# A three-layer interaction network with an MLP on one Trainium2 core: products and sums of layer 0 spread over four tiles, MLP parts known early moved ahead, and a head issued from two queues

## The reference

```python
def _cin_layer(X0, Xi, W, b):
    H = W.shape[0]
    F0_, Fi = (X0.shape[1], Xi.shape[1])
    Wr = W.reshape(H, F0_, Fi)
    return jnp.einsum('hjk,bjd,bkd->bhd', Wr, X0, Xi) + b[None, :, None]
...
e = jnp.stack([tbl_0[ids[:, 0]], ...], axis=1)      # (512, 39, 16)
X0 = Xi = e
for W, b in Ws:
    Xi = _cin_layer(X0, Xi, W, b)
    res.append(Xi.sum(axis=2))
z = jnp.concatenate(res, axis=1)                      # (512, 384)
h = jnp.concatenate([z, dense_ctx], axis=1)
h = jnp.maximum(h @ W_top1 + b_top1, 0.0)
h = jnp.maximum(h @ W_top2 + b_top2, 0.0)
y = h @ W_top3
```

## Time and profile before

| | us |
|---|---|
| median of three runs | 722.71 |
| the profiled execution, as timed | 718.87 |
| its span in the trace | 717.1 |
| TensorE busy | 671.6 (94%) |
| ScalarE busy | 541.1 (75%) |
| VectorE busy | 469.7 (66%) |
| GpSimd busy | 460.5 (64%) |

### The profile page before, as it was taken

How to read it: one execution, slowest core, us unless ns; L and a number is a source line. 1 busy time by engine, 2 the same in 40 slices (tenths; PEclk the granted TensorE clock), 3 DMA queues, 4 the chain that set the end, 5 groups by cost and what they waited for, 6 DMA issues and landing times. The chain is left out here.

```text
span 717.1 us, 10090 instructions
## 1 busy us (share of the span) xinstructions
PE 671.6 (94%) x2631; PEld 481.9 (67%) x2631; DVE 469.7 (66%) x954; ACT 541.1 (75%) x1939; POOL 460.5 (64%) x445
## 2 busy tenths in 40 slices
PE   4597999999999999999999999999999999998998
PEld 4464777777677767676767677776777776774443
DVE  6245677778677777777676777786777777784000
ACT  4255797979797979888897979797979798993003
POOL 6765686877778686868686868777785736321000
PEclk9699999999999999999999999999999999998999
DMA  6664040404031312213040404040313122300000
GB/s 202 220 176 97 1 99 1 98 1 98 2 95 6 92 8 73 26 41 59 16 84 3 98 2 97 2 97 3 96 4 93 5 79 91 143 1 0 0 1 0
DMA packets 103772, 41.40 MB, mean 58 GB/s; under 512 B 86961, under 2 KB 90033, under 8 KB 103074
## 3 DMA queue, kind: packets, MB, share of 16 engines
q1 hardware_dynamic: 98594, 39.47, 21.7%
q0 software_dynamic: 5120, 1.29, 2.2%
HBM read 11.29 MB, written 2.59 MB: 19 GB/s over the span
## 5 line engine op out<-in xcount | busy, mean ns | idle before, releaser
L415 ACT ACTIVATE prod<-ps_y,xt 128x128 f32<-128x128 f32 x1792 | 498.1, 452 | 88.0 <-PE ps_y L659 79.4
L657 PE MATMUL ps_y<-w_hi,x_hi 128*128 128x512 f32 (+1 forms) x640 | 307.9, 481 | 16.2 <-DVE prod L529 14.4
L323 POOL TENSOR_TENSOR prod<-prod 128x512 f32<-128x512 f32 x128 | 165.6, 1294 | 133.6 <-ACT prod L415 132.0
L659 PE MATMUL ps_y<-w_hi,x_lo 128*128 128x512 f32 (+1 forms) x640 | 249.2, 389 | 0.0
L658 PE MATMUL ps_y<-w_lo,x_hi 128*128 128x512 f32 (+1 forms) x640 | 248.9, 389 | 0.0
L529 DVE SCALAR_TENSOR_TENSOR prod<-ps_y,xt,prod 128x128 f32<-128x128 f32 x576 | 163.8, 343 | 48.0 <-PE ps_y L659 46.2
L298 POOL DMA_INDIRECT rows<-in_table,index x160 | 153.4, 959 | 42.7 <-issue 35.7
L657 PEld LDWEIGHTS ps_y<-w_hi,x_hi 128*128 128x128 f32 x640 | 120.8, 189 | 72.3 <-DVE prod L529 26.3
L536 DVE TENSOR_REDUCE prod<-prod 128x128 f32<-128x1536 f32 x64 | 112.2, 1753 | 85.3 <-ACT prod L415 53.0
L658 PEld LDWEIGHTS ps_y<-w_lo,x_hi 128*128 128x128 f32 x640 | 120.8, 189 | 47.1 <-issue 25.5
L659 PEld LDWEIGHTS ps_y<-w_hi,x_lo 128*128 128x128 f32 x640 | 120.5, 188 | 25.3
(11 more groups left out here) (62 smaller groups left out, 235.9 us busy)
## 6 DMA issues: line engine op xcount, KB each, us to landing
room<-room SPq DMA_DIRECT2D x80, 234.0 KB
room<-room SPq DMA_DIRECT2D x48, 78.0 KB
emb_room<-rows SPq DMA_DIRECT2D x180, 5.0 KB
rows<-in_table,index POOLq DMA_INDIRECT x160
g_all<-in_L_rec_W SPq DMA_DIRECT2D x1, 2496.0 KB, 9.8
room<-room SPq DMA_DIRECT2D x16, 156.0 KB
w2t_dram<-g_all SPq DMA_DIRECT2D x1, 2496.0 KB
room<-w2t_dram SPq DMA_DIRECT2D x1, 2496.0 KB, 8.9
```

The source lines that it names most:

```text
L323: nc.gpsimd.tensor_tensor(prod[:, SLOT[a]:SLOT[a] + 2], prod[:, SLOT[a]:SLOT[a] + 2], prod[:, SLOT[b]:SLOT[b] + 2], ALU.add).then_inc(pool ...
L415: ins = nc.scalar.activation(prod[:, SLOT[k] + m // 2, :, m % 2], ps_y[:, g % YBANKS, m * H:(m + 1) * H], ACT.Copy, scale=xt[:, q % 2, ti, ...
L657: nc.tensor.matmul(y, hi, w1_hi[:, cols], start=True, stop=False)
L659: nc.tensor.matmul(y, lo, w1_hi[:, cols], start=False, stop=True).then_inc(y_made, 1)
```

## The change

- **Layer 0 beside the tiles.** The seven sums on TensorE were one in tile 1, five in tile 2 and one in tile 3; now they are one, two, two and two. GpSimd's products move ahead with them, the first two into tile 0. Four gathers of tile 0 are spread over tiles 0 to 2. The shares have a semaphore of their own, so the first product waits for them alone.
- **Tail.** Two of the four parts of the first MLP layer need nothing of layer 1. They now have their accumulators in four banks. For two of these the matmuls go behind group 3 of tiles 60 to 63, for the two others right behind tile 63. The part with layer 1's output goes behind the 39 matmuls with W2. The second layer runs both halves for three inputs first and then for the fourth. The bias of `r1` is added after tile 60.
- **Head.** ScalarE's queue issues half of the first lay-outs, shares and windows. W2 is loaded in two parts, the first ahead of the small loads, and turned in three lots: five groups before the rows are turned, three after, two behind layer 0. GpSimd repeats the rows of quad 1 ahead of the last three gathers of quad 2.

```diff
-MULTIPLIED_IN = {(1, 0): range(0, 1), (1, 1): range(1, 4), (2, 0): range(4, 5), (2, 1): range(5, CHUNKS)}
-GATHERED_IN = {(0, 0): range(0, 1), (0, 1): range(1, 5), (3, 0): range(5, 6), (3, 1): range(6, GATHERS)}
+MULTIPLIED_IN = {(0, 1): range(0, 2), (1, 0): range(2, 3), (1, 1): range(3, 4), (2, 0): range(4, 5),
+                 (2, 1): range(5, CHUNKS)}
+GATHERED_IN = {(0, 0): range(0, 1), (0, 1): range(1, 2), (1, 1): range(2, 4), (2, 1): range(4, 5),
+               (3, 0): range(5, 6), (3, 1): range(6, GATHERS)}
 REPEATED_IN = (2, 1)
-SUMMED_AFTER = {(1, 8): 0, (2, 0): 1, (2, 2): 2, (2, 4): 3, (2, 6): 4, (2, 9): 5, (3, 1): 6}
+
+SUMMED_AFTER = {(0, 9): 0, (1, 4): 1, (1, 9): 2, (2, 3): 3, (2, 8): 4, (3, 0): 5, (3, 2): 6}
 SUM_D_AFTER = 6
+
+MLP_AFTER = {(0, 3): (0, 0), (1, 3): (1, 0), (2, 3): (0, 1), (3, 3): (1, 1)}
...
+PREP_EARLY = PREP - PREP_W2 + PREP_W2 // 2
+PREP_LATE = PREP - 2
...
+        ps_h1 = [ps_tr[:], ps_x1[:], ps_y[:, 0, :], ps_y[:, 1, :]]
+        ps_r3 = ps_y[:, 2, :]
+        ps_h2 = [ps_y[:, 3, :], ps_y[:, 4, :]]
+        ps_out = ps_g[0:1, :]
...
+            sp.dma_start(w2_in[:, W1_PARTS[0]], W2[:, W1_PARTS[0]]).then_inc(w2_ld[0], 16)
...
-            lay_out(0)
-            sp.dma_start(w2_in, W2).then_inc(w2_ld, 16)
+            lay_out(0, range(FPG // 2))
+            sp.dma_start(w2_in[:, W1_PARTS[1]], W2[:, W1_PARTS[1]]).then_inc(w2_ld[1], 16)
+
             sp.wait_ge(x0_made, 1)
-            share_rows(0, first_shared)
-            for c in range(1, CHUNKS):
-                cut_window(0, c, first_window[c])
-            lay_out(1)
+            share_part(sp, 0, 0, first_shared)
+            share_part(sp, 0, 2, first_shared)
+            for c in range(2, CHUNKS, 2):
+                cut_part(sp, 0, c, first_window[c])
+            lay_out(1, range(FPG // 2))
...
             def multiply(q, c):
                 if c == 0:
-                    wait(pool, shifted[q % 2], 16 * MOVES * ((q + 1) // 2))
+                    wait(pool, shared[q % 2], 16 * SPC * ((q + 1) // 2))
+                    wait(pool, z_used, CHUNKS * (q - 1) + 1)
+                if c == 1:
+                    wait(pool, cut[q % 2], 16 * (CHUNKS - 1) * ((q + 1) // 2))
                 r = chunk_rows(c)
                 window = bz[0:r, c, :] if c else x0[0:r, q % 2, :]
-                if c == 0:
-                    wait(pool, z_used, CHUNKS * (q - 1) + 1)
                 nc.gpsimd.tensor_tensor(bz[0:r, c, :], window, xa[0:r, :], ALU.mult).then_inc(z_made, 1)
...
             for g in range(GATHERS):
+                if g == GATHERS - 3:
+                    repeat_rows(1)
                 gather(2, g)
-            repeat_rows(1)
...
+            act.wait_ge(gathered[0], 16 * GATHERS)
+            for f in range(FPG // 2, FPG):
+                lay_out_part(act, 0, f)
+            for n in range(PREP - PREP_W2, PREP_EARLY):
+                keep_prep(n)
             keep_x0(0)
+            act.wait_ge(x0_made, 1)
+            share_part(act, 0, 1, first_shared)
+            for c in range(1, CHUNKS, 2):
+                cut_part(act, 0, c, first_window[c])
             keep_xt(0)
-            for n in range(PREP - PREP_W2, PREP):
+            for n in range(PREP_EARLY, PREP_LATE):
                 keep_prep(n)
+            act.wait_ge(gathered[1], 16 * GATHERS)
+            for f in range(FPG // 2, FPG):
+                lay_out_part(act, 1, f)
             keep_x1(0)
+            for n in range(PREP_LATE, PREP):
+                keep_prep(n)
...
+                if T == TILES - QT:
+                    dve.wait_ge(bsum_made, 1)
+                    dve.wait_ge(r1_made, QUADS)
+                    nc.vector.tensor_scalar(r1[:], r1[:], b02_sum[:, 0:1], None, ALU.add).then_inc(r1_done, 1)
             reduce_late(TILES - 1)
-            dve.wait_ge(bsum_made, 1)
-            dve.wait_ge(r1_made, QUADS)
-            nc.vector.tensor_scalar(r1[:], r1[:], b02_sum[:, 0:1], None, ALU.add).then_inc(r1_done, 1)
...
-            for n in range(PREP - PREP_W2):
+            for n in range(PREP_EARLY):
                 turn_prep(n)
             turn_rows(0)
             turn_x(0)
-            for n in range(PREP - PREP_W2, PREP):
+            for n in range(PREP_EARLY, PREP_LATE):
                 turn_prep(n)
             for c in range(CHUNKS):
                 layer0(0, c)
+            for n in range(PREP_LATE, PREP):
+                turn_prep(n)
```

On TensorE, the new function and the tail:

```diff
+            def known_mlp1(m, part):
+                if (m, part) == (0, 0):
+                    pe.wait_ge(late_mlp, 64)
+
+                    pe.wait_ge(bd_made, QUADS)
+                    pe.wait_ge(x1_lo_made, QUADS)
+                    pe.wait_ge(r1_made, QUADS)
+                if (m, part) == (0, 1):
+                    pe.wait_ge(r1_done, 1)
+                w, z = (wt1[0:C, 3, m * P:(m + 1) * P], dense_t[:]) if part == 0 else (wt1[:, 0, m * P:(m + 1) * P], r1[:])
+                nc.tensor.matmul(ps_h1[m], w, z, start=part == 0, stop=False)
...
-            def mlp1(c, rows_c, z, start, stop):
-                for m in range(MC1):
-                    ins = nc.tensor.matmul(ps_y[:, m, :], wt1[0:rows_c, c, m * P:(m + 1) * P], z,
-                                           start=start, stop=stop)
-                    if stop:
-                        ins.then_inc(h1_summed, 1)
-
-            pe.wait_ge(late_mlp, 64)
-            pe.wait_ge(act_step, ACT_STEPS * TILES)
-            pe.wait_ge(dve_step, DVE_STEPS * TILES)
-            mlp1(3, C, dense_t[:], True, False)
-            pe.wait_ge(r1_done, 1)
-            mlp1(0, P, r1[:], False, False)
+                    if not nxt and (ti, g) in MLP_AFTER:
+                        known_mlp1(*MLP_AFTER[ti, g])
+
+            for m in range(2, MC1):
+
+                if m == 2:
+                    pe.wait_ge(dve_step, DVE_STEPS * (TILES - 1) + DVE_DONE[YBANKS])
+                else:
+                    pe.wait_ge(act_step, ACT_STEPS * (TILES - 1) + ACT_GROUPS.index(YBANKS + 1) + 1)
+                for part in range(2):
+                    known_mlp1(m, part)
             sum_d(TILES - 1)
             pe.wait_ge(late_w2, 16)
             pe.wait_ge(g_kept, TILES)
-            mlp1(1, P, g_all[:, F, :], False, False)
+            pe.wait_ge(act_step, ACT_STEPS * TILES)
             for j in range(F):
-                ins = nc.tensor.matmul(ps_x1[:], w2t[:, j * H:(j + 1) * H], g_all[:, j, :],
-                                       start=j == 0, stop=j == F - 1)
+                ins = nc.tensor.matmul(ps_r3, w2t[:, j * H:(j + 1) * H], g_all[:, j, :], start=j == 0, stop=j == F - 1)
             ins.then_inc(r3_summed, 1)
+            for m in range(MC1):
+                nc.tensor.matmul(ps_h1[m], wt1[:, 1, m * P:(m + 1) * P], g_all[:, F, :], start=False, stop=False)
             pe.wait_ge(r3_made, 1)
-            mlp1(2, P, r3, False, True)
-            for m in range(MC2):
-                dst = ps_y[:, YBANKS - 1, :] if m == 0 else ps_g[:]
-                for c in range(MC1):
-                    if m == 0:
-                        pe.wait_ge(h1_made, c + 1)
-                    ins = nc.tensor.matmul(dst, wt2[:, c, m * P:(m + 1) * P], h1[:, c, :],
-                                           start=c == 0, stop=c == MC1 - 1)
-                ins.then_inc(h2_summed, 1)
+            for m in range(MC1):
+                nc.tensor.matmul(ps_h1[m], wt1[:, 2, m * P:(m + 1) * P], r3, start=False,
+                                 stop=True).then_inc(h1_summed, 1)
+            for half in (range(MC1 - 1), range(MC1 - 1, MC1)):
+                for m in range(MC2):
+                    for c in half:
+                        if m == 0:
+                            pe.wait_ge(h1_made, c + 1)
+                        ins = nc.tensor.matmul(ps_h2[m], wt2[:, c, m * P:(m + 1) * P], h1[:, c, :],
+                                               start=c == 0, stop=c == MC1 - 1)
+                    if MC1 - 1 in half:
+                        ins.then_inc(h2_summed, 1)
             for m in range(MC2):
                 pe.wait_ge(h2_made, m + 1)
-                ins = nc.tensor.matmul(ps_tr[0:1, :], wt3[:, m:m + 1], h2[:, m, :], start=m == 0, stop=m == MC2 - 1)
+                ins = nc.tensor.matmul(ps_out, wt3[:, m:m + 1], h2[:, m, :], start=m == 0, stop=m == MC2 - 1)
             ins.then_inc(y_summed, 1)
```

60 lines of the change are left out of this document (33 added, 27 removed).

## The result

The changed kernel takes 736.88 us (median of 4, 734.58 to 738.55), the kernel before beside it 722.08: a ratio of 1.0206 (95% interval 1.0183 to 1.0230): slower, by 1.8 to 2.3%. I had forecast 723.2 and a range of 717 to 729: wrong, by 13.7 us. The direction I had called the likeliest came, but not the size.

A forecast was written before the change was run, and what follows sets the result against it. TensorE was taken to bound the full tiles, ScalarE the four last tiles. 718.87 - 2.2 (head and first quad) + 10.9 (steady quads) - 8.2 (tail) = 719.4; the median 3.84 above gave 723.2 us, range 717 to 729.

The forecast's parts named there:

- the clock rival: Steady quads: 2 us waits lower the granted clock for 4 us, 1.6 more per quad, 745.6 us; chance 0.05.
- The wait, 2.03 + 0.1 us for +0.77 a quad: Steady quads: TensorE waits 2.03 us for GpSimd's first product, 0.1 for restart; the old 1.36 goes, net +0.77.
- waits of 1.26 show 1.00 throughout: Steady quads: the argument against the clock rival, that the granted clock held at 1.00 with waits of 1.26 us.
- my own "for": Tail: the argument for the clock rival, that the clock fell there after 2.1 us and thin work.
- 22.3: Head: turning of the rows was to start at 22.3 us instead of 23.28, with lay-outs issued from two queues.
- the third rival: Head: transfers, not issues, limit it; product at 38.6 instead of 36.7, 1.9 later, 725.1 us; chance 0.12.
- The gain of 3.4: Head: tile 0 was to start at 41.3 us instead of 44.70, through issuing from two queues.
- The other rival, slow issues on ScalarE: Head: eight issues at 1.4 us instead of 0.7 start tile 0 5.2 later, 728.4; decides from 0.95; chance 0.10.
- 45.4: First quad: 45.4 us instead of 44.2, with a 6.0 us wait for the first product instead of 5.03.
- -10.4 and +2.2: Tail: 45.3 us behind the last quad instead of 55.7 (-10.4); four last tiles 32.8 instead of 30.6 (+2.2).
- 0.86 for all eight: Tail: each first-MLP-layer matmul of two passes, in the last tiles or behind them, costs 0.86 us.
- the terms' span: Whole kernel: terms gave 719.4 us including 1.8 around the span; 3.84 more, the old median's excess, gave 723.2.

The follow-up runs named there:

- e3: Changed kernel with one gather moved from ahead of the second addition and first product to behind the products: 717.86 us, ratio 0.9954 to the kernel before.
- after: The changed kernel itself, as described under the change, against the kernel before: 736.88 us, ratio 1.0206.
- e4: Changed kernel with an idle memset on GpSimd ahead of each first product: 749.59 us, ratio 1.0389 to the kernel before.
- h3: h1 with the head of the kernel before (SyncE issues all, W2 late and turned in one lot): 698.95 us, ratio 0.9678.
- h2: h1 with SyncE issuing all first lay-outs, shares and windows, W2 still early: 699.38 us, ratio 0.9701.
- h1: g1's kernel unchanged, run again on a fourth chip: 696.96 us, ratio 0.9646 to the kernel before; the best version.
- e1: Changed kernel with the three tables of products, gathers and sums as before the change: 709.79 us, ratio 0.986 to the kernel before.
- s1: e1 with GpSimd's first product waiting for windows as well as shares, as before the change: 728.68 us, on a chip with a late tile 0.
- g3: g1 with W2 loaded in one piece behind the lay-outs and turned in one lot, ScalarE still issuing half: 715.19 us, ratio 0.9612.
- g1: Changed kernel, first sum three groups later, old product and sum tables in the first quad, dense context's 16 rows padded to 128: 713.5 us, ratio 0.9591.

## Why the prediction was wrong

**Steady quads: the failed step is the clock rival.** The wait, 2.03 + 0.1 us for +0.77 a quad, was right: the quad came within 0.03. I then gave a fall of the clock behind it a chance of 0.05, because "waits of 1.26 show 1.00 throughout". That is no evidence on a wait of 2.1: it lay between 1.26, after which the clock had held, and 5.03, after which it had fallen, and my own "for" named a fall after 2.1 us in the tail. e3, after and e4 put the border just there: 0, 8 and 11 of 12. (The trace counts the first and the new one as 1.10 and 1.85 of idle time; that changes nothing in the order.) What the runs showed instead: a fall in 8 of 12 quads at 1.6 us each, 12.8 us. The price I had (1.6 a fall) was right; 8 of 14 on top of the forecast would have been 736.0. The forecast did all the sums and chose the wrong case.

**Head.** Turning began at 23.58, not 22.3: the small loads (the dense rows and `b_row` last), issued behind the new half load of W2 and 3.4 to 3.6 us later than before, kept TensorE waiting for 1.31 us, so ScalarE's lay-outs started at 19.67 instead of 18.6. SyncE's started late too, at 19.27 instead of 18.20, although the gathers ahead of them were issued 0.4 earlier. With W2 late (h3) SyncE starts at 17.76 and TensorE doesn't wait; with it early it starts at 18.55 (h2) and 18.71 (h1). ScalarE was free at 31.7, not 30.0: its share took 1.39 and its windows 0.83 each. The products did not run on end but until 39.7, with two waits for transfers (0.99 and 0.81 us; the DMA share from 34 to 38 is 0.90). This is the third rival (its 38.6). The Trainium skill says in the place cited there ("DMA: Bandwidth & Descriptors", Issuing engines are not separate DMA queues) that issuing from several engines saves only the time of issuing; these two waits agree with it. But they didn't set the end of the sums, since TensorE had no idle time between its passes. What did is that the sums began at 34.16, some 1.5 us later than the forecast had them (39.5 less 6.18 and 0.7 is 32.6), and ran at half clock until shortly before 39, so that they took 8.55 instead of 6.18, where I had allowed 0.7. The gain of 3.4 became 0.25. The other rival, slow issues on ScalarE, came close in its price (0.95 us for a late lay-out, the point named) and didn't decide: its last issue ended at 39.4 and the sums at 42.7, 3.3 us later.

**First quad.** 44.96 for 45.4, by luck in part: the wait was 5.32 for 6.0, with half clock behind it as said. That the split semaphore and ScalarE's lay-outs for the second quad are worth 4 us with the old tables (e1, s1, h2; with W2 turned in lots, g3) stood nowhere in the forecast: it let the first product wait for the shares alone, but never asked what that alone is worth with the old tables. In the changed kernel the early demand of its tables used it up.

**Tail.** -10.4 and +2.2 were forecast, -9.65 and +3.6 came. The mis-sized term is the matmuls on 16 rows among those on 128, where I took 0.86 for all eight: the two in the tiles took 1.25 each, and the four behind tile 63 (two of them on 16 rows) 4.1 instead of 3.4. That is 1.4 of the 2.1, and g1 with 128 rows removes it. Most of the rest is 0.5 in tile 60, where TensorE waits 0.24 us for VectorE and restarts.

**The place on the scale.** The median was taken 5.6 us above the terms' span, from the kernel before; it was 2.4. The traced execution of the kernel before was one of its shorter ones: it had a mean clock of 0.983, and on two other chips the kernel before took 718.1 us at 0.983 and 722.3 to 724.0 at 0.976.

## What to carry to other kernels

A rival that is tested only by waits shorter than the one you are adding has not been tested: price the clock's fall as soon as the new wait is longer than any after which the trace shows the clock holding. When the point at which a consumer asks is moved forward, look at what stands ahead of the producer on its queue: here three groups later, one entry of a table, were worth 32.6 us. And an edit to what a wait counts, or to who issues a transfer, is worth tracing to the next stage: both gains of this head arise 10 to 20 us after it.

## What the runs showed of the hardware

- An idle stretch of TensorE of 1.25 us once in 38 us left the granted clock at 1.00 in 12 of 12 quads, one of 1.85 was followed by the lower level in 8, one of 2.33 in 11. Each fall cost the quad 1.6 us. Single waits of 2.29 and 2.44 left it up.
- A matmul of two passes over 16 rows among those over 128 took 1.25 us of a tile, one over 128 rows with zeros in 112 of them 0.86. Six passes over 16 rows one behind the other took 0.44 each, so the mixture costs, not the rows.
- DMAs issued by ScalarE took 0.63 to 0.71 us for a first lay-out, 0.83 for a window and 1.39 for a share, against 0.69, 0.8 and 0.86 on SyncE. While both queues issued later lay-outs, each took 0.95 on either (eight in 7.6 us); SyncE alone took 0.67 (16 in 10.71, h2). An instruction of ScalarE behind four such issues came 3.99 us late (the copy of xt).
- On two of four chips tile 0 started at 56.07 to 67.90 us instead of 43.6 to 49.0, in waits marked "issue" and "remote" between turned banks. What causes it stays open: no run was made on it, and the kernel before wasn't traced there.
